# Keys kept in fp32 per chunk and split per group; projection weights double-buffered through an on-chip copy

## The reference

```python
q, k, v = (einsum('blh,dh->bdl', u, W) + b for W, b in ((Wq, bq), (Wk, bk), (Wv, bv)))
k  = causal_conv(k, k_kernel) + k_D * k          # by FFT in the reference
kv = k * v
y  = (causal_conv(kv, ssm_kernel) + D * kv) * q
x  = layernorm(u + (y @ Wo.T + bo))
h  = square(relu(x @ W_fc.T));  y2 = h @ W_proj.T   # 1024 hidden
x  = layernorm(x + spikes(y2) / 5)                  # 5 steps of a threshold recurrence
```

## Time and profile before

| | |
|---|---|
| median of 3 runs | 899.39 us (898.63 to 899.83) |
| profiled execution | 902.56 us, its span 900.8 us |
| PE busy | 753.9 us (84%) |
| DVE busy | 778.5 us (86%) |
| ACT busy | 517.2 us (57%) |
| POOL busy | 400.9 us (45%) |
| front, convolution loop, rest | 0 to 76, 76 to 438, 438 to 901 us |

### The profile page before, as it was taken

How to read it: one execution, slowest core, us unless ns; L and a number is a source line. 1 busy time by engine, 2 the same in 40 slices (tenths; PEclk the granted TensorE clock), 3 DMA queues, 4 the chain that set the end, 5 groups by cost and what they waited for, 6 DMA issues and landing times.

```text
span 900.8 us, 26648 instructions
## 1 busy us (share of the span) xinstructions
PE 753.9 (84%) x11392; PEld 554.1 (62%) x11392; DVE 778.5 (86%) x1157; ACT 517.2 (57%) x560; POOL 400.9 (45%) x307
## 2 busy tenths in 40 slices
PE   0078978788878988867469999999999999999993
PEld 0078978788778988867445555555545555555541
DVE  6887889887878789999757899999999999999885
ACT  2396666666665666633335656555666555666562
POOL 0352112222222222211346876666876666786542
PEclk9999999999998899976669999999999999999997
DMA  9985888876878787676110011111011111001001
GB/s 336 335 218 146 205 197 190 195 187 159 199 181 190 182 190 154 144 167 181 48 48 1 1 48 47 47 47 47 0 47 47 47 47 47 21 26 48 24 23 47
DMA packets 55614, 101.59 MB, mean 113 GB/s; under 512 B 5728, under 2 KB 41440, under 8 KB 53600
## 3 DMA queue, kind: packets, MB, share of 16 engines
q1 hardware_dynamic: 54144, 97.94, 41.7%
q10 hardware_dynamic: 1376, 2.23, 0.7%
HBM read 89.92 MB, written 27.01 MB: 130 GB/s over the span
## 4 chain that ended last, share of the span: by engine, by line
PE 38%; DVE 31%; POOL 15%; issue 12%; DMA 3%; ACT 1%; SPq 1%; POOLq 0%; DVEq 0%; ACTq 0%
PE ps L725 13%; POOL arena L671 13%; PE ps L747 12%; DVE arena L1211 7%; PE ps L842 5%; PE ps L849 4%; DVE arena L1055 2%; DVE u_maxima L943 2%; DVE arena L1168 2%; DVE arena L1208 2%; PE ps L823 2%; DVE arena L1187 2%; DMA arena<-kpad_dram 2%; DVE arena L1193 1%; DVE arena L996 1%
## 5 line engine op out<-in xcount | busy, mean ns | idle before, releaser
L501 ACT ACTIVATE arena<-arena 64x3584 f16<-64x3584 f16 x60 | 191.3, 3189 | 124.2 <-DVE arena L1035 123.5
L725 PE MATMUL ps<-arena 128*128 128x96 f16 x3072 | 147.6, 213 | 68.7 <-DVE arena L996 50.7
L747 PE MATMUL ps<-arena 128*128 128x64 f16 (+2 forms) x5088 | 151.7, 184 | 43.4 <-issue 23.7
L725 PEld LDWEIGHTS ps<-arena 128*128 128x128 f16 x3072 | 142.1, 102 | 71.7 <-issue 60.2
L671 POOL TENSOR_TENSOR arena<-arena 128x512 f16<-128x512 f32 x128 | 178.9, 1429 | 14.7 <-ACT arena L553 14.2
L747 PEld LDWEIGHTS ps<-arena 128*128 128x128 f16 x5088 | 147.3, 99 | 46.3 <-issue 40.6
L849 PE MATMUL ps<-arena 128*128 128x512 f16 x768 | 173.2, 379 | 2.8 <-POOL arena L671 2.8
L842 PE MATMUL ps<-arena 128*128 128x512 f16 x768 | 170.8, 379 | 0.9 <-issue 0.9
L635 POOL TENSOR_TENSOR arena<-arena 128x512 f16<-128x512 f32 x32 | 40.4, 1262 | 278.9 <-ACT arena L507 278.9
L1200 DVE TENSOR_TENSOR arena<-arena 128x512 f32<-128x512 f32 x128 | 137.7, 1129 | 10.4 <-POOL arena L671 9.0
L549 ACT ACTIVATE arena<-ps,read_factor 128x512 f32<-128x512 f32 x128 | 87.9, 687 | 79.4 <-PE ps L842 62.4
(11 more groups left out here) (106 smaller groups left out, 868.1 us busy)
## 6 DMA issues: line engine op xcount, KB each, us to landing
arena<-kpad_dram SPq DMA_DIRECT2D x166, 256.0 KB, 5.2
kpad_dram<-ksplit_dram SPq DMA_DIRECT2D x64, 256.0 KB, 5.6
qy<-in_uT SPq DMA_DIRECT2D x8, 1024.0 KB, 17.3
arena<-in_u SPq DMA_DIRECT2D x16, 512.0 KB, 4.2
out<-arena SPq DMA_DIRECT2D x16, 512.0 KB, 3.0
qy<-kpad_dram SPq DMA_DIRECT2D x22, 256.0 KB, 6.5
arena<-in_k SPq DMA_DIRECT2D x2, 512.0 KB, 4.8
ksplit_dram<-arena ACTq DMA_DIRECT2D x2, 512.0 KB, 3.7
```

What stands on the lines that cost most here:

```text
L501: nc.scalar.activation(*shifted(windows1_of(s, half)), ACT.Copy).then_inc(c1_copied, 1)
L725: last = nc.tensor.matmul(o, u16[:, x, t, tok:tok + P], wcur[:, r, w, t], start=(k == 0), stop=(k == 3 * DT - 1))
L747: last = nc.tensor.matmul(out[:, ch * COL + delta * B:(ch + 1) * COL], win[:, delta * P:(delta + 1) * P], data(xp, ch)[:, 0:cols], start=( ...
```

## The change

- `ktmp` and the two-chunk `k16` go. `kbuf` holds two chunks of k in fp32, stored quarter after quarter; `k16` now holds two *groups* in two parts. ACT and POOL split group g+1 in step g (groups 0 to 31, so up to step 30), behind the kv part; one split, of group 0, stands ahead of the loop instead of four. The splits read the four quarters of a group (`keys_of`) and write them interleaved by sequence (`by_quarter`).
- ACT's split waits for all four reads of the chunk (`proj_read`) and for conv1 of g-2; DVE no longer waits for POOL (`k_lo`) before it reads a projection; conv1 of g waits for the split of g.
- `wcur` is a single buffer. The next chunk's weights are loaded to `wnext`, and DVE copies `wnext` to `wcur` (128x384 fp16) behind the read of the last quarter of each chunk, seven times. PE's first `project` of a chunk and SP's next weight load wait for that copy (`wcur_ready`).
- ACT's loop is unrolled over all 32 steps.

```diff
-        k16 = part(16, F16, "p (r a n) -> p r a n", r=2, a=2)
+        kbuf = part(16, F32, "p (r q n) -> p r q n", r=2, q=GPC)
-        wcur = part(1.5, F16, "p (r a t n) -> p r a t n", r=2, a=2, t=DT)
+        wcur = part(0.75, F16, "p (a t n) -> p a t n", a=2, t=DT)
+        wnext = part(0.75, F16, "p (a t n) -> p a t n", a=2, t=DT)
-        ktmp = part(4, F32, "p (r n) -> p r n", r=2)
+        k16 = part(4, F16, "p (r a n) -> p r a n", r=2, a=2)
...
+        def keys_of(s):
+            n = s % GPC * (GC // GPC)
+            return kbuf[:, s % PAIR // GPC, :, n:n + GC // GPC].rearrange("p q (m b) -> p q m b", b=4)
+        def by_quarter(a):
+            return a.rearrange("p (m q b) -> p q m b", q=GPC, b=4)
...
 (SP)
-                    sp.wait_ge(proj, GPC * (chunk - 1))
-                    load_w(chunk, chunk % 2)
+                    sp.wait_ge(wcur_ready, 2 * (chunk - 1))
+                    load_w(chunk, wnext, ld_wnext)
...
 (ACT)
-            def k_part(quarter, r, n):
-                act.wait_ge(ktmp_ready, n + 1)
-                nc.scalar.activation(quarter_of(k16[:, r, 0], quarter), dense(ktmp[:, quarter % 2]), ACT.Copy
-                                     ).then_inc(k_hi, 1)
+            def k_part(g):
+                act.wait_ge(proj_read, GPC * (g // GPC + 1))
+                if g >= 2:
+                    act.wait_ge(c1_half, 2 * (g - 2) + 2)
+                nc.scalar.activation(by_quarter(k16[:, g % 2, 0]), keys_of(g), ACT.Copy).then_inc(k_hi, 1)
...
-                if more:
-                    k_part(s % GPC, (s // GPC + 1) % 2, base + s + GPC)
+                if g + 1 < NG:
+                    k_part(g + 1)
...
+            for half in range(2):
+                copy_windows(0, 0, half)
+            k_part(0)
+            for g in range(NG):
+                step(g % PAIR, g)
...
 (POOL)
+            def k_part(s, g):
+                pool.wait_ge(k_hi, g + 1)
+                nc.gpsimd.tensor_tensor(by_quarter(k16[:, s % 2, 1]), keys_of(s), by_quarter(k16[:, s % 2, 0]),
+                                        ALU.subtract).then_inc(k_lo, 1)
...
-                if more:
-                    k_part(s % GPC, (s // GPC + 1) % 2, base + s + GPC)
+                if not (isinstance(base, int) and base + s == NG - 1):
+                    k_part(s + 1, base + s + 1)
...
 (PE)
-                    if s % GPC == 0:
-                        pe.wait_ge(ld_wcur[(s // GPC + 1) % 2], (pair + s // GPC + 1) * 16)
+                    if g % GPC == 0:
+                        pe.wait_ge(wcur_ready, 2 * (g // GPC + 1))
...
-                conv1(s, g, base + (s // GPC + 1) * GPC)
+                conv1(g, g)          # waits k_lo >= g + 1
...
 (DVE, read_projection)
-                if not isinstance(n, int) or n >= 2:
-                    dve.wait_ge(k_lo, n - 1)
...
+                if quarter == GPC - 1 and chunk + 1 < NC:
+                    dve.wait_ge(ld_wnext, 16 * (chunk + 1))
+                    nc.vector.tensor_copy(wcur, wnext).then_inc(wcur_ready, 2)
```

More of the change, by code:

```diff
@@ L216, in build @@
             sem(n) for n in ("c1_copied_dve", "c1_half", "c2_half", "c2_widened"))
-        ld_wcur = [sem(f"ld_wcur{r}") for r in range(2)]
-        proj, proj_read, ktmp_ready, k_hi, k_lo = (sem(n) for n in ("proj", "proj_read", "ktmp_ready", "k_hi", "k_lo"))
+        ld_wcur, ld_wnext, wcur_ready = (sem(n) for n in ("ld_wcur", "ld_wnext", "wcur_ready"))
+        proj, proj_read, k_hi, k_lo = (sem(n) for n in ("proj", "proj_read", "k_hi", "k_lo"))
         kv_ready, kv_hi, kv_lo, y_ready = (sem(n) for n in ("kv_ready", "kv_hi", "kv_lo", "y_ready"))
@@ L357, in load_windows, with load_w @@
                                      ).then_inc(t_in[g % 2 * 2 + half], 16)
[L359 to L363, removed]
+            def load_w(chunk, dst, done):
+                sp.dma_start(dst.rearrange("p a t x -> p (a t x)"),
+                             w16_dram[:, chunk:chunk + 1].rearrange("p c a x -> p (c a x)")).then_inc(done, 16)
             sp.wait_ge(w16_out, 16)
-            load_w(0, 0)
-            load_w(1, 1)
+            load_w(0, wcur, ld_wcur)
+            load_w(1, wnext, ld_wnext)
             sp.wait_ge(kpad_zero, 1)
@@ L501, in copy_windows, with step @@
                 nc.scalar.activation(*shifted(windows1_of(s, half)), ACT.Copy).then_inc(c1_copied, 1)
[L503 to L506, removed]
+            def step(s, g):
+                if g + 1 < NG:
+                    copy_windows(s + 1, g + 1, 0)
+                act.wait_ge(kv_ready, g + 1)
                 nc.scalar.activation(kv16[:, s % 2, 0], vbuf[:, s // GPC, group_of(s):group_of(s) + GC], ACT.Copy
                                      ).then_inc(kv_hi, 1)
-                if more:
-                    k_part(s % GPC, (s // GPC + 1) % 2, base + s + GPC)
[L511 to L524, removed]
+                if g + 1 < NG:
+                    k_part(g + 1)
+                if g + 1 < NG - GPC:
+                    copy_windows(s + 1, g + 1, 1)
+            for half in range(2):
[3 more added lines that the diff above has]
+                step(g % PAIR, g)
             def y_turn(i):
@@ L647, in _ @@
                 split_u(n)
-            for quarter in range(GPC):
-                k_part(quarter, 0, quarter)
+            k_part(0, 0)
             phase1(pool, step)
@@ L713, in _, with project @@
         def _(pe):
-            def project(quarter, r, n, banks=PA, before=0):
+            def project(quarter, n, banks=PA, before=0):
                 if not isinstance(n, int) or n > before:
@@ L725, in project @@
                                 last = nc.tensor.matmul(o, u16[:, x, t, tok:tok + P],
-                                                        wcur[:, r, w, t],
+                                                        wcur[:, w, t],
                                                         start=(k == 0), stop=(k == 3 * DT - 1))
@@ L752, in convolve @@
                     last.then_inc(done, 1)
-            pe.wait_ge(ld_wcur[0], 16)
+            pe.wait_ge(ld_wcur, 16)
             for quarter in range(GPC):
@@ L760, in _, with conv1 @@
                     pe.wait_ge(u_lo_pool, by_pool)
-                project(quarter, 0, quarter, PAS[quarter % 2], 1)
-            def conv1(s, g, k_ready):
-                pe.wait_ge(k_lo, k_ready)
+                project(quarter, quarter, PAS[quarter % 2], 1)
+            def conv1(s, g):
+                pe.wait_ge(k_lo, g + 1)
                 if not isinstance(g, int) or g >= 2:
                     pe.wait_ge(kv_ready, g - 1)
-                convolve(0, PC1[:, s % 2], lambda a, ch: k16[:, s // GPC, a,
-                                                             group_of(s) + ch * COL:group_of(s) + (ch + 1) * COL],
+                convolve(0, PC1[:, s % 2], lambda a, ch: k16[:, s % 2, a, ch * COL:(ch + 1) * COL],
                          lambda half, c, a: windows1_of(s, half)[:, c, a], g + 1, c1_half)
@@ L778, in conv2, with step @@
                          g + 1, c2_half)
-            def step(s, base, more, pair, first=False):
-                g = base + s
-                if more:
-                    if s % GPC == 0:
-                        pe.wait_ge(ld_wcur[(s // GPC + 1) % 2], (pair + s // GPC + 1) * 16)
-                    project(s % GPC, (s // GPC + 1) % 2, g + GPC, PA, int(first))
-                if first:
-                    pe.wait_ge(proj_read, GPC)
-                conv1(s, g, base + (s // GPC + 1) * GPC)
[L790 to L798, removed]
+            def step(g):
+                if g < NG - GPC:
+                    if g % GPC == 0:
+                        pe.wait_ge(wcur_ready, 2 * (g // GPC + 1))
+                    project(g % GPC, g + GPC, PA, int(g == 0))
+                if g == 0:
+                    pe.wait_ge(proj_read, GPC)
+                conv1(g, g)
+                if g:
+                    conv2(g - 1, g - 1)
+            for g in range(NG):
+                step(g)
+            conv2(NG - 1, NG - 1)
             def turn(src, done):
@@ L1001, in read_projection @@
                 dve.wait_ge(proj, n + 1)
-                if not isinstance(n, int) or n >= 2:
-                    dve.wait_ge(k_lo, n - 1)
                 tiles = banks.rearrange("p i (b x) -> p x (i b)", b=4)
-                for s, dst in ((0, dense(ktmp[:, quarter % 2])), (1, quarter_of(vbuf[:, r], quarter)),
+                for s, dst in ((0, kbuf[:, r, quarter]), (1, quarter_of(vbuf[:, r], quarter)),
                                (2, quarter_of(qy[:, bass.ds(chunk * CH * COL, CH * COL)], quarter))):
```

8 lines of the change are left out of this document (2 added, 6 removed).

## The result

| | before | after |
|---|---|---|
| median | 900.00 us (10 runs, 898.6 to 903.5) | 908.15 us (10 runs, 902.2 to 912.6) |
| profiled execution, its span | 902.56, 900.8 | 905.68, 903.5 |

The ratio is 1.0078 (1.0050 to 1.0106), so the change costs 7.0 us (4.5 to 9.5). Forecast was 905.8 (900.4 to 909.2): slower by 6.4. A second set of runs of the changed kernel gave 1.0076 (1.0050 to 1.0103). Single executions spread over some 10 us (902.2 to 912.6 for the changed kernel; 895.8 to 907.9 for the kernel before in the 25 executions beside r_after), and the two profiled ones are only 2.7 us of span apart. The change's 7.0 us can't be read off one pair of traces; what follows takes differences between stretches of a trace only where several traces repeat them.

A forecast was written before the change was run, and what follows sets the result against it. PE and DVE were taken to hold each other up in the convolution loop, with no one bound. Terms 2.4 + 0.75 + 3.3 gave +6.4 us on the 899.39 us median: 905.8 us, range 900.4 to 909.2.

The forecast's parts named there:

- Three of the signs: Trace signs: shift of 2.4 to 3 us to step 20, loop end 6 us later; stalls differing several us meant wrong.
- Part 1: Before the loop: PE's first project waits for DVE's last read and the weight copy, starting at 71.99, +2.4 us (2.2 to 2.8).
- u's last split: Before the loop: DVE's last split of u gains nothing from POOL's removed key splits (ends 0 and 1.0 us).
- Rival (b): No change that can be told: PE's 27.0 us of unexplained stalls shrink when PE is held elsewhere, about 900.3, chance 0.15.
- Part 2: Six later chunk changes: PE's project waits for DVE's weight copy, +0.75 us (0.3 to 4.1).
- The count of three: At three of the six chunk changes PE starts on DVE's read, so only three copies cost 0.25 us each.
- Part 3: Steps 28 to 30 each gain a key split; POOL's operation delays DVE's copies by 1.1 us each, +3.3 us (0 to 3.9).
- the upper end: Last steps: PE's convolutions, held for POOL's split, could come late for DVE by up to 1.2 us a step; none counted.
- (a): POOL's operations in the last steps fit beside DVE's PSUM reads or waits, leaving only the weight costs: 902.5, chance 0.17.
- (c): Faster: shifted window loads remove a third of PE's unexplained stalls, 9 us, giving 896.8, chance 0.07.
- (d): Last steps cost PE time too, or the per-step split binds mid-loop: +3.9 us or more, 909.7 and up, chance 0.09.
- (e): ACT's unrolled loop, had its loop been the hidden cost, changes no number: still 905.8; no chance given.

The follow-up runs named there:

- r_after: The changed kernel timed and traced once more, with no further edit: ratio 1.0076 to the kernel before, 6.8 us slower (4.5 to 9.3).
- h1: Changed kernel with weights in two buffers again and without POOL's low key part of groups 29 to 31: -0.4 us to the kernel before (-2.0 to 1.4).
- e3: Changed kernel without POOL's low key part of groups 29 to 31, that computation left out: +2.2 us to the kernel before (0.3 to 4.0).
- e2: Changed kernel with the weights back in two buffers and no copy on DVE: +4.6 us to the kernel before (2.3 to 6.8).
- e4: Kernel before with only ACT's loop unrolled over all 32 steps: -0.6 us to the kernel before (-3.1 to 1.8).
- g1: Changed kernel with weights in two buffers and the low key part of groups 29 to 31 on DVE, not POOL: +4.6 us to the kernel before (2.3 to 7.0).
- f2: Kernel before with unread filler matmuls on PE in step 1 and in the waits of steps 28 to 31: +1.5 us to the kernel before (-0.1 to 3.1).
- e1: Kernel before with only PE's first project in the loop waiting for all four reads instead of three: +3.0 us to the kernel before (0.9 to 5.0).
- g3: Changed kernel with three more weight copies at each of the six chunk changes inside the loop: +12.1 us to the kernel before (8.4 to 15.8).
- f1: Changed kernel with unread filler matmuls on PE before the projects of steps 0 and 1: +6.6 us to the kernel before (4.0 to 9.2).

## Why the prediction was right, and where it was off

**The direction and the sum.** 6.4 us foreseen, 7.0 measured (4.5 to 9.5), at the two places named, the weights and the tail, with no third that can be seen (h1). By the pairs above the two parts are 2.5 and 4.9 us, 7.4 together, where the terms were 3.15 (2.4 + 0.75) and 3.3; with 2 us to either side the times neither confirm nor refute the terms singly. The traces do better, and show terms of the wrong size: the front shifts by 3.9 us and not 2.4, and the tail grows by 3.8 made of 2.3 and 1.5 and not of 3.3 and 0. That the sum came within 0.6 us is partly luck.

Three of the signs didn't come as named. The shift didn't stay at 2.4 to 3 us up to step 20: it was 4.9 to 5.5 at step 2 and -0.2 and 1.4 at step 20 in the two traces. The loop's last times_v came 2.6 us later in the first trace and 5.5 in the second, for 6. PE's stalls without a cause differed by 6.4 us, which was named as a sign of being wrong.

**Part 1, the front, +2.4.** The mechanism, the start of PE (0.1 us off), the copy and the absence of a gain from u's last split (L990 takes 4.32 us as before) were right. The shift was mis-sized: the term took the project behind the wait at full speed. That came true in one trace of the five with this wait (e3, 4.25 us and 2.4 us of shift). In the other four the clock fell to 0.50 after PE's 2.1 to 2.2 us of waiting and added 1.5 us at once, so the shift was 3.9 to 4.2 us at step 0 in the changed kernel. Another 1.0 to 1.2 by step 2 is the clock of step 1, 0.72 for 0.86; e2 and h1 have that too without the wait (1.2 and 1.1 us between steps 0 and 1), so it isn't shown to be the wait's.

Rival (b) said that PE's stalls without a visible cause would shrink and pay the shift back. They are fewer in both traces of the changed kernel (20.6 and 22.6 us for 27.0), and between steps 2 and 28 these traces win back 6.1 and 4.0 us. But this isn't the wait's doing as far as the record shows: kernels without the wait have as few such stalls (e4 21.6 us, h1 21.8) and win as much against the one trace of before in the same steps (e4 3.3, g1 3.7, h1 4.8, f2 3.2), and e1, which has the wait and nothing else, has 28.5 us of stalls and wins 0.4. The one trace of before is rather a slow one there: 11 of the 13 others win against it. Whether any of the front's 4 to 5 us is paid back stays open: its 2.5 us in time has 2 to either side.

**Part 2, the six copies, +0.75.** The count of three was wrong: PE waited for the copy at five of the six changes, and at all six in the second trace (3.2 and 2.4 us in all, part of it for the read in front of the copy), and at five in g3. The price of one was right in the median (0.25), with 0.99 and 0.88 us for two of them, beside POOL:

```profile
L1015 DVE COPY arena<-arena x7: 240/249/989, 71.6 to 342.5; 128x384 f16<-128x384 f16 x7
```

The weights' whole part is known to 2 us only, so this one can't be given its own size from the times.

**Part 3, the tail, +3.3.** That three key splits come into steps where DVE never rests was right, and that POOL beside L1055 and L1059 costs DVE about the length of an operation: 1.06 us in step 28, 0.95 in step 29 (L1051 and L1055 now). In step 30 POOL ran beside the masks (1.55 us for 1.30) and before the copies (2.22 and 2.09 as before). So DVE's part was 2.3 us and not 3 x 1.1 = 3.3. The step that failed is the one that put PE's lateness at none: it was 0.5 us in step 29 and 1.0 more than before in step 30, within the 1.2 us a step that I had named as the upper end. The start of conv1(29), foreseen at 403.9, was right: it came at 402.66 in a trace that is 1.2 us ahead at step 28. That the second of the two convolutions behind it would run at full speed was the reason for counting none; the two took 6.20 us, where two short ones take 5.3 and two long ones 6.9. The tail is 3.8 to 4.0 us longer in two traces, 4.9 (some 2 to either side) in time.

**The rivals.** (a), a covered tail, is out by e3 and h1. (c), faster, is out. (d) had two halves. That the tail costs PE time too came true, at 1.5 us and not the 3.9 or more that (d) asked for; that the split one step ahead binds in the middle is out as a cost by h1, though PE did wait for it there twice (1.14 us at 155.88, 0.84 at 347.90). (e), ACT's loop, is out as a cost by e4. What stays open, besides the paying back: which of PE's stalls without a visible cause an execution has, and with it the 10 us between executions. Even the half behind the loop, which no edit touches, takes 473.0 to 476.2 us in these traces.

## What to carry to other kernels

A wait put in front of a busy PE can cost more than its length, since the granted clock can fall behind it (here 2.2 us of waiting became a shift of 3.9, in four traces of five): look at the granted clock of the stretch behind each new wait. A piece of work moved from "several steps ahead" to "one step ahead" was free here in the steady state (to 1.4 us) and reappeared at the loop's end, where its cover has gone; count the operations per step in the last steps. Price it by what it stands beside, not by its own engine's idle time: POOL was busy for 15% of that stretch, and its operation cost DVE about a microsecond in two steps of three. And where executions differ by 10 us, take each reading of one trace to several others, those without the change too, before calling it an effect of the change.

## What was not expected of the hardware

- The granted clock of PE fell from 1.00 to 0.50 behind a wait of 2.1 to 2.2 us that followed 4.25 us of work without a pause, in four of the traces with this wait (both of the changed kernel, e1, g3), and not in e3 (1.00 from 72 to 78 us, and a shift of 2.9 for 3.9 at step 0). It stayed at 1.00 in f1, where matmuls filled the wait. In the first trace of the changed kernel it was 0.50 from 71.8 us on with the DMA share at 0.00, so the transfers aren't its cause.
- With fillers that kept the clock up, stalls without a visible cause stood in other places and were up to 3.1 us long (2.95 us at 101.24), 27.0 us in f1 and 34.5 in f2 for 20.6 and 27.0 without fillers, and neither of the two kernels with them was faster. That the fillers cause these stalls isn't shown: e1 has 28.5 us of them without any.
- A DVE operation on SBUF of 0.25 us took up to 0.99 us, and one of 0.67 us took 1.34, where POOL had started first. The Trainium skill ("SBUF — State Buffer", SBUF: two separate sides) calls this an exclusive lock held for the whole instruction; these durations agree with it.
